# Edge stage of a graph kernel: flat visit loops, the carried sums added by VectorE, a later attention product, and TensorE's first query products ahead of the second gates

## What is computed

```python
q, k, v = x_norm @ Wq.T + bq, x_norm @ Wk.T + bk, x_norm @ Wv.T + bv
dk = silu(edge_attr @ Wdk.T + bdk)
dv = silu(edge_attr @ Wdv.T + bdv)
attn = sum(q[dst] * k[src] * dk, axis=1)
attn = silu(attn) * cosine_cutoff(edge_weight)
agg = segment_sum(v[src] * dv * attn[:, None], dst)
out = x + agg @ Wo.T + bo
```

## Time and profile before

| | |
|---|---|
| median of 3 runs | 2702.92 us (2702.91 to 2708.73) |
| the profiled execution | 2704.13 us |
| its span, first to last instruction | 2702.6 us |
| PE busy, share of the span | 2347.1 us, 87% |
| DVE busy | 2231.1 us, 83% |
| ACT busy | 1899.4 us, 70% |
| POOL busy | 1725.5 us, 64% |

### The profile page before, as it was taken

The page is one execution under the profiler, slowest core; times in us unless marked ns, Lnnn a source line. Parts: engine busy times, 40 slices in busy tenths (PEclk is TensorE's granted clock), DMA queues, the critical chain, the costliest instruction groups (busy, mean ns, idle before and its releaser), DMA issues. The chain is left out here.

```text
span 2702.6 us, 55102 instructions
## 1 busy us (share of the span) xinstructions
PE 2347.1 (87%) x12558; PEld 1931.7 (71%) x12559; DVE 2231.1 (83%) x6310; ACT 1899.4 (70%) x4106; POOL 1725.5 (64%) x1829
## 2 busy tenths in 40 slices
PE   5446686999999999999999999999999999999975
PEld 4323344888888777887778788787778888887864
DVE  4276667998988888898989898898889899898965
ACT  1234334878878777887778777778787888887844
POOL 3343205777777777777777777777776777777723
PEclk8768788999999999999999999999999999999987
DMA  9646536999999999999999999999898999999943
GB/s 298 183 71 164 167 133 192 271 268 275 270 268 271 266 265 266 268 273 263 267 264 268 270 270 267 269 272 267 262 272 263 270 274 269 272 269 270 268 151 116
DMA packets 318259, 662.33 MB, mean 245 GB/s; under 512 B 79334, under 2 KB 131666, under 8 KB 318224
## 3 DMA queue, kind: packets, MB, share of 16 engines
q0 software_dynamic: 137824, 446.91, 57.6%
q1 hardware_dynamic: 172272, 205.20, 25.8%
q10 hardware_dynamic: 8128, 9.90, 1.1%
HBM read 602.50 MB, written 59.30 MB: 245 GB/s over the span
## 5 line engine op out<-in xcount | busy, mean ns | idle before, releaser
L966 POOL DMA_INDIRECT e_kv<-kv_tab,e_idx x1604 | 1565.9, 976 | 602.9 <-issue 475.7
L1089 ACT ACTIVATE e_gate_ps<-e_gate_ps 128x1024 f32<-128x1024 f32 x802 | 811.6, 1012 | 431.9 <-PE e_gate_ps L1022 431.2
L1161 DVE TENSOR_TENSOR e_gated<-e_kv,e_gate_ps 128x1024 f32<-128x1024 f32 x804 | 974.4, 1212 | 16.8 <-DMA e_kv<-kv_tab,e_idx 15.8
L1006 PE MATMUL e_sum_ps<-e_gated,e_weighed_hot 128*128 128x256 f32 x3232 | 837.7, 382 | 99.4 <-issue 97.2
L1021 PE MATMUL e_gate_ps<-wd_hi_lo,e_high 128*128 128x512 f32 x1604 | 745.3, 465 | 31.1 <-DVE e_gated L1161 30.5
L1006 PEld LDWEIGHTS e_sum_ps<-e_gated,e_weighed_hot 128*128 128x128 f32 x3232 | 583.1, 190 | 195.4 <-issue 114.9
L1022 PE MATMUL e_gate_ps<-wd_bias,e_low 128*128 128x512 f32 x1604 | 634.6, 396 | 0.0
L1171 DVE CUSTOM_DVE_ANT_0 e_gated<-e_gated,e_q_ps 128x256 f32<-128x256 f32 x1608 | 603.3, 410 | 2.9 <-PE e_q_ps L1041 2.1
L1099 ACT ACTIVATE e_weighed_hot<-e_hot,e_attn 128x128 f32<-128x128 bf16 x1612 | 524.3, 399 | 0.5 <-DVE e_attn L1183 0.5
L1040 PE MATMUL e_q_ps<-e_q_win,e_hot_t 128*128 128x256 f32 x1604 | 401.0, 283 | 11.9 <-issue 10.9
L1041 PE MATMUL e_q_ps<-e_q_win,e_hot_t 128*128 128x256 f32 x1604 | 397.6, 281 | 0.0
(11 more groups left out here) (145 smaller groups left out, 1632.8 us busy)
## 6 DMA issues: line engine op xcount, KB each, us to landing
e_attr<-attr_groups_dram SPq DMA_DIRECT2D x800, 128.0 KB
e_kv<-kv_tab,e_idx POOLq DMA_INDIRECT x1604
e_q_win<-q_tab SPq DMA_DIRECT2D x100, 256.0 KB
sum_tab<-e_sums SPq DMA_DIRECT2D x102, 128.0 KB
e_prior<-sum_tab SPq DMA_DIRECT2D x101, 128.0 KB
q_tab<-l_q_out SPq DMA_DIRECT2D x50, 256.0 KB, 6.0
kv_tab<-l_kv_out SPq DMA_DIRECT2D x50, 256.0 KB, 6.2
xt_tab<-xt_out SPq DMA_DIRECT2D x50, 132.0 KB, 3.6
```

Of the source, the lines that this page charges most:

```text
L966: pool.indirect_dma_start(kv[:, k, :], None, kv_tab, bass.IndirectOffsetOnAxis(ap=idx[:, k:k + 1], axis=0)).then_inc(kv_landed[k // G][k % ...
L1006: last = nc.tensor.matmul(sum_ps[:, 0:H], weighed_hot[:, c % 2, k, :], gated[:, c * G + k, H:2 * H], start=(c == 0 and k == 0), stop=False)
L1089: nc.scalar.activation(gate_ps[:, 2 * p:2 * p + 2, :], gate_ps[:, 2 * p:2 * p + 2, :], ACT.Silu).then_inc(silu_ready[s][p], 1)
L1161: nc.vector.tensor_tensor(gated[:, pair(s, p), :], kv[:, pair(s, p), :], gate_ps[:, 2 * p:2 * p + 2, :], ALU.mult).then_inc(gated_ready[s] ...
```

## The change

All engines but SP and DVE walk one flat loop over all visits; its length, `total`, is computed once by DVE in the set-up. DVE and SP keep the nested loops, since they need the block and the window. PE steps its wait registers ahead of the visit's last `gather_q`. The product with the identity leaves PE, `take_sums` leaves ACT, and DVE adds the carried rows to the sums in one instruction in group 3, which then waits for the landing of `e_prior`. `attend(c)` moves behind `gate_rows(c, 1)`. In group 0, `e_place` is made behind `gate_rows(0, 0)`, and `one_hot(0)` behind `dot_rows(0, 0)`. `one_hot` and the second `gate_rows` get waits of their own, which were implied before. On PE, `gather_q(c, 0)` moves in front of `gates(c, 1)`. SP's stream is as before.

```diff
+                    then(nc.vector.tensor_copy(spread[:], spread_i[:]))
+                    then(nc.vector.tensor_reduce(further[:], spread[:], AX.X, ALU.add))
+                    nc.vector.tensor_scalar(total[:], further[:], float(BLOCKS), None, ALU.add)
...
+    def of_last(self, c, lag):
+
+        assert c >= lag
+        return self.prev
...
+        def all_visits(eng):
+            return eng.value_load(total[0:1, 0:1], min_val=BLOCKS, max_val=BLOCKS * -(-N // P))
...
-                with pool.Fori(0, BLOCKS) as t:
-                    n = visits(pool, t)
-                    with pool.Fori(0, n):
-                        gather_half(0)
-                        gather_half(1)
-                        visit.step()
+                with pool.Fori(0, all_visits(pool)):
+                    gather_half(0)
+                    gather_half(1)
+                    visit.step()
...
-                                                start=(c == 0 and k == 0), stop=False)
-                    if c == GROUPS - 1 and p == 1:
-                        pe.wait_ge(prior_landed, visit.now16)
-                        last = nc.tensor.matmul(sum_ps[:, 0:H], ident[:], prior[:], start=False, stop=True)
+                                                start=(c == 0 and k == 0), stop=(c == GROUPS - 1 and k == G - 1))
...
-                with pe.Fori(0, BLOCKS) as t:
-                    n = visits(pe, t)
-                    with pe.Fori(0, n):
-                        for c in range(GROUPS):
-                            segment_sum(c, 0)
-                            gates(c, 0)
-                            segment_sum(c, 1)
-                            turn_hot(c)
-                            gates(c, 1)
-                            gather_q(c, 0)
-                            gather_q(c, 1)
-                        visit.step()
+                with pe.Fori(0, all_visits(pe)):
+                    for c in range(GROUPS):
+                        segment_sum(c, 0)
+                        gates(c, 0)
+                        segment_sum(c, 1)
+                        turn_hot(c)
+                        gather_q(c, 0, visit.of)
+                        gates(c, 1)
+                        of = visit.of
+                        if c == GROUPS - 1:
+                            visit.step()
+                            of = visit.of_last
+                        gather_q(c, 1, of)
...
-                def take_sums():
-                    act.wait_ge(summed[GROUPS - 1], visit.prev)
-                    act.wait_ge(stored, visit.now16)
-                    nc.scalar.copy(sums[:], sum_ps[:, 0:H]).then_inc(sums_ready, 1)
-
...
+                with act.Fori(0, all_visits(act)):
+                    for c in range(GROUPS):
+                        silu_of_dot(c)
+                        round_attr(c)
+                        silu(c, 0)
+                        weigh(c)
+                        copy_hot(c)
+                        silu(c, 1)
+                    visit.step()
...
-                    if p == 0:
-                        dve.wait_ge(silu_ready[s][p], visit.of(c, 2))
+                    dve.wait_ge(silu_ready[s][p], visit.of(c, 2))
...
+                    dve.wait_ge(weighed_ready[c][1], visit.prev)
...
+                def take_sums():
+
+                    dve.wait_ge(stored, visit.now16)
+                    dve.wait_ge(go, 1)
+                    dve.wait_ge(prior_landed, visit.now16)
+                    dve.wait_ge(summed[GROUPS - 1], visit.prev)
+                    nc.vector.tensor_tensor(sums[:], sum_ps[:, 0:H], prior[:], ALU.add).then_inc(sums_ready, 1)
...
-                        dve.wait_ge(hot_ready[GROUPS - 1], visit.prev)
-                        nc.vector.tensor_scalar(place[:], dst_f[:, bass.ds(t * BLOCK_TILES, BLOCK_TILES)], window_f[:, bass.ds(t, 1)],
-                                                steps[:, bass.ds(r, 1)], ALU.subtract, ALU.subtract).then_inc(place_ready, 1)
                         for c in range(GROUPS):
                             gate_rows(c, 0)
+                            if c == 0:
+                                dve.wait_ge(hot_ready[GROUPS - 1], visit.prev)
+                                nc.vector.tensor_scalar(place[:], dst_f[:, bass.ds(t * BLOCK_TILES, BLOCK_TILES)], window_f[:, bass.ds(t, 1)],
+                                                        steps[:, bass.ds(r, 1)], ALU.subtract, ALU.subtract).then_inc(place_ready, 1)
+                                dot_rows(c, 0)
+                                one_hot(c)
+                            else:
+                                one_hot(c)
+                                dot_rows(c, 0)
+                            gate_rows(c, 1)
                             attend(c)
-                            one_hot(c)
-                            dot_rows(c, 0)
-                            gate_rows(c, 1)
                             low_attr(c)
+                            if c == GROUPS - 1:
+                                take_sums()
                             dot_rows(c, 1)
```

More of the change, by code:

```diff
@@ L425, in gnn_kernel @@
         edge_stage(nc, dict(
[L426 removed]
+            ident_bf=ident_bf, iota=iota, steps=steps, src_tiles=src_tiles, dst_f=dst_f, cut=cut, window_f=window_f, walk=walk, total=total,
             wd_hi_lo=wd_hi_lo, wd_bias=wd_bias, q_tab=q_tab, kv_tab=kv_tab, sum_tab=sum_tab, attr_groups=attr_groups,
@@ L830, in edge_stage @@
 def edge_stage(nc, shared):
-    ident, ident_bf, iota, steps, src_tiles, dst_f, cut, window_f, walk, wd_hi_lo, wd_bias = (
-        shared[n] for n in ("ident", "ident_bf", "iota", "steps", "src_tiles", "dst_f", "cut", "window_f", "walk", "wd_hi_lo", "wd_bias"))
+    ident_bf, iota, steps, src_tiles, dst_f, cut, window_f, walk, total, wd_hi_lo, wd_bias = (
+        shared[n] for n in ("ident_bf", "iota", "steps", "src_tiles", "dst_f", "cut", "window_f", "walk", "total", "wd_hi_lo", "wd_bias"))
     q_tab, kv_tab, sum_tab, attr_groups, NP, N, BLOCKS = (
@@ L1030, in turn_hot, with gather_q @@
                     last.then_inc(turned[c], 1)
-                def gather_q(c, p):
+                def gather_q(c, p, of):
                     s = slot(c, 1)
                     if p == 0:
-                        pe.wait_ge(hot_t_ready[s], visit.of(c, 1))
+                        pe.wait_ge(hot_t_ready[s], of(c, 1))
                         if s == 0:
                             pe.wait_ge(q_landed, visit.now16)
-                    pe.wait_ge(dotted[slot(c, 2)][p], visit.of(c, 2))
+                    pe.wait_ge(dotted[slot(c, 2)][p], of(c, 2))
                     for k in (2 * p, 2 * p + 1):
@@ L1062, in _ @@
                             gates(c, p)
-                            gather_q(c, p)
+                            gather_q(c, p, visit.of)
             @block.scalar
@@ L1106, in copy_hot @@
                     nc.scalar.copy(hot_t[:, c % 2, :, :], hot_ps[:, 0:G, :]).then_inc(hot_t_ready[c], 1)
-                def take_sums():
-                    act.wait_ge(summed[GROUPS - 1], visit.prev)
-                    act.wait_ge(stored, visit.now16)
-                    nc.scalar.copy(sums[:], sum_ps[:, 0:H]).then_inc(sums_ready, 1)
                 act.wait_ge(dve_ready, 1)
                 nc.scalar.preload_act_table(ACT.Silu)
[L1115 to L1118, removed]
-                            silu_of_dot(c)
-                            round_attr(c)
-                            silu(c, 0)
-                            weigh(c)
-                            copy_hot(c)
-                            if c == GROUPS - 1:
-                                take_sums()
-                            silu(c, 1)
-                        visit.step()
+                with act.Fori(0, all_visits(act)):
[7 more added lines that the diff above has]
+                    visit.step()
                 for c in range(GROUPS - 1):
@@ L1133, in _ @@
                     weigh(c)
-                take_sums()
             @block.vector
             def _(dve):
-                visit = Visits(dve, "dve_e", "cur prev now32 late32")
+                visit = Visits(dve, "dve_e", "cur prev now16 now32 late32")
                 preset(dve, low_ready, 0)
```

5 lines of the change are left out of this document (4 added, 1 removed).

## The result

The changed kernel is slower: 2770.05 us median of 6 runs (2750.78 to 2778.16), where the kernel before took 2702.8 us beside it (6 runs, 2692.15 to 2708.73). The ratio is 1.0249, with a 95% interval from 1.021 to 1.0288. The profiled execution is the longest of the six, with a span of 2776.4 us, against 2702.6 before.

A forecast was written before the change was run, and what follows sets the result against it. PE was taken to set the pace at 21.51 us a visit; fixed steps of 17.12 plus a 3.70 landing gave 20.82. With 0.63 saved a visit, 62 us, the forecast was 2641 us, range 2600 to 2706.

The forecast's parts named there:

- rival C: Landing of `e_q_win` bounds the loop and lengthens to 4.9 us under denser gathers: 22.0 us a visit, 2753 us; chance 0.12.
- The landing: Group 1: `e_q_win` lands 3.70 us after issue, and PE's early query products wait for it.
- The fixed part: PE's visit apart from the landing of `e_q_win`: 17.12 us.
- DVE is slack: DVE needs 20.0 us a visit with its added sum and 0.3 us loop turn, less than PE, so costs nothing.
- The turn of the loop on PE: Between last query product and next visit's first sum: flat loop saves 0.80 us a visit, 0.13 stays.
- the new stall: PE in group 1, before the first query products: 1.3 to 1.4 us each visit, total wait some 100 to 140 us.
- The idle at `e_sum_ps`: PE's idle in front of its sums was to fall from 73 us to under 20.
- The DMA share: Busy share of the DMA engines in the edge loop, 93% before, was to be 0.95 or more.
- The third sign: The prediction would be wrong if DVE waited for key and value rows (`e_kv`) more than 30 us.
- A: Gathers and DMA engines take back 0.2 to 0.35 us a visit through late key and value rows: 2661 to 2690 us; chance 0.17.
- B: Load of `e_q_win` lands earlier or is hidden, saving 1.2 us a visit until POOL bounds it: 2585 us; chance 0.08.
- D: No gain: PE's loop turn stays, or DVE's 20.0 us of work and new place hold PE; 2703 to 2712 us; chance 0.13.

The follow-up runs named there:

- e3: The kernel before with only the new order, first query products ahead of the second gates in all groups: 2859.65 us, 1.06 of before.
- e2: The changed kernel with the old order of second gates and first query products in group 1 alone: 2650.2 us, 0.9823 of before.
- e6: The kernel before with flat loops on PE, ACT and POOL and nothing else, on a slower chip: 0.9856 of before there.
- e8: e2 with PE's two nested loops back, on a slower chip: 0.9513 of before there.
- e4: The changed kernel with twelve unread products on PE in group 1, between transposes and first query products: 2728.17 us, 1.0104 of before.

## Why the prediction was wrong

It said 2641 us, range 2600 to 2706, with 0.75 for faster. It came to 2770, outside the range, on the side of rival C. The sum was 20.82 us a visit. The measured visit is 22.28 us in the mean of 99, 1.46 more, and three terms make this up. One was sized too low, and two were put at nothing.

- **The landing: +0.55.** I took 3.70 and it was 4.25 (3.96 and 4.83 in the two kinds of visits). The mechanism, a sum of fixed part and landing, held (slope 0.92); the size was too low. Rival C named this, with the mean near 4.9 and through denser gathers on fuller DMA engines. The direction is right, the reason is not shown: the landing is 4.1 to 4.25 us in all five kernels with an edit that ran on chips at 2700 us, `e3` among them, while the engines' share in the loop was 0.88 (after), 0.86 (`e3`) and 0.94 (`e2`). How full the engines are does not set it, neither over the loop nor just then: in the 3.5 us behind the issue their share is 0.92 in before and 0.84 in after. The Trainium skill's rule for C ("DMA: Bandwidth & Descriptors", section Latency and other measured facts: HBM's latency grows under load) doesn't explain it in this form, since the load was lower in after. What does set it stays open.
- **The fixed part: +0.42.** I had 17.12 and visits with a steady clock show 17.54. The step that failed is that DVE is slack. PE's timeline, cut at the first sums of each group, shows where it went (means in us; 99 visits of each kernel):

  | kernel, visits | group 0 | group 1 | group 2 | group 3 |
  |---|---|---|---|---|
  | before, 99 | 4.88 | 5.53 | 4.84 | 6.26 |
  | after, clock stays, 67 | 5.41 | 6.46 | 4.82 | 4.81 |
  | after, clock falls, 32 | 5.40 | 8.35 | 5.38 | 4.81 |

  Group 3 gave 1.45, a little more than I took off it (4.81 against 4.97). But group 0, which the sum left as it was, grew by 0.53. DVE's own turn of the nested loop, which I took at 0.3 us and left off the path, is 0.61 us between its last dots and the next gate rows; `gates(0, 0)` on PE waits for those gate rows. DVE's timeline of after at the turn:

```profile
1506.07 0.42 DVE L1169 CUSTOM_DVE_ANT_0 e_gated<-e_gated,e_q_ps 128x256 f32<-128x256 f32 x1
...
1507.10 1.22 DVE L1159 TENSOR_TENSOR e_gated<-e_kv,e_gate_ps 128x1024 f32<-128x1024 f32 x1 [0.61 <-issue]
1508.24 0.34 DVE L1210 TENSOR_SCALAR e_place<-dst_f,window_f,steps 128x16 bf16 x1
```

  The same turn in before, on DVE and on PE:

  ```profile
  1508.24 0.29 DVE L1202 TENSOR_SCALAR e_place<-dst_f,window_f,steps 128x16 bf16 x1 [0.32 <-issue]
  1508.45 1.21 DVE L1161 TENSOR_TENSOR e_gated<-e_kv,e_gate_ps 128x1024 f32<-128x1024 f32 x1
  ...
  1510.35 0.58 PE L1021 MATMUL e_gate_ps<-wd_hi_lo,e_high 128*128 128x512 f32 x1
  ```

  In before the gate rows end at 1509.66, 0.69 us ahead of the gates: that was the margin. In after they end at 1508.32, and PE's gates start at 1508.47, 1.23 us behind their sums (1507.24), where in before it was 0.75 us (1509.60 to 1510.35). Over all visits the two are 1.21 and 0.75. So some 0.5 us of what the flat loop saved on PE came back as a wait in front of the next gates: as long as PE turned slowly, DVE's turn lay under PE's. This is read from the two traces; the runs that were to show it by their times (`e6`, `e8`) fell on the other chips. The waits view had shown me only how little PE waited for DVE there, not by how little DVE was ahead. I had priced DVE's line at 20.0 us a visit against 20.8 and stopped there; the margin to look at was the one at the turn.
- **The clock: +0.50.** Nothing in the prediction spoke of it. The earlier trace rows show it at 1.00 all through the loop, and I let it stand for the new kernel, in which PE would stand 1.3 to 1.4 us in each visit by my own sum, and more in the visits with late landings. In 32 of 99 visits the fixed part is 19.10 instead of 17.54: 32/99 x 1.56 = 0.50. `e4` takes it away and gets some 40 us back, where 0.50 x 99 is 50. The Trainium skill ("TensorE: Matmul & The Clock Gate", section Terms) prices a throttled stretch at its length times the share of pulses left out; for the 109 us at half rate that is an estimate of 55 us, a little above the 50 of the table and the 40 of `e4`.

0.55 + 0.42 + 0.50 is 1.47, against the 1.46 to be explained. One small reading was off as well and is in none of the three: the transposes of the earlier trace rows end at 1517.15 + 0.39 = 1517.54, not at 1517.35, so that a landing of 3.7 us meant a stall of 1.2 us, not 1.3 to 1.4.

**What held.** The turn of the loop on PE is gone, wholly: from the last query product of a visit to the next sum it is 0.12 us (0.13 more was to stay, so the saving is over the 0.80 taken). The identity's product is gone, the wait at `e_attn` too, and the new stall is in group 1, in each visit. It was forecast at 100 to 140 us and is 170.6. The idle at `e_sum_ps` went as forecast. The savings came to 0.89 together (`e3` against after), not 1.36; most of the difference, 0.47, is DVE's turn again (`gates(0, 0)` start 0.75 us behind their sums in `e3`, 1.21 in after).

**The signs named ahead.** The DMA share was to rise to 0.95 or more and fell to 0.88, and the period is over 21.4: both say that the prediction fell. The third sign, late key and value rows, stayed low in after; it appeared in `e2`, where PE is fast enough.

**The other rivals.** A (the transfers take part back) was priced at 0.2 to 0.35 us a visit on top of a gain. Its signs are in `e2`, another kernel than the one it was made for: landings of 4.1 us and key and value rows late three times as often, at 2650 us. B (an early landing) found no support: none of these five has a mean under 4.1. The prediction's 2.6 us for this size is an estimate from a fit that the Trainium skill ("DMA: Bandwidth & Descriptors", section Anatomy of one DMA) gives for DMAs on GpSimd's path; this load is issued by SP, so the fit was stretched to it, and 3.7 to 4.25 was measured among the gathers. C's 2753 us is the price nearest to the result, but by luck in part: its landing of 4.9 was not reached in the mean, and two terms that it did not have make up the rest. D's second half, DVE as the holder, is the 0.42, through its turn and not through its 20.0 us of work.

The point where I chose wrong is the one where I took 3.7 with a break-even at 4.4 and gave C 0.12. With the real fixed part the break-even was 21.51 - 17.54 = 3.97 us, a quarter of a microsecond over the mean I had read, and the loss beyond it is steeper than 1 to 1, because the clock fell behind most of the longest stalls.

## What to carry to other kernels

Before work is moved away from between a load's issue and its first use, take the distribution of the landing, not its mean, and ask what the stall costs beyond its own length: on PE stalls of 1.9 to 2.9 us were followed by a halved clock in 32 of 99 visits. Where one engine's loop turn is removed, look at the others' turns, since they may have lain under it. A reordering that is good in three of four groups (13 us here) can lose in the fourth (115 us), so it is applied group by group, where the data are there already.

## What the runs showed of the hardware

- The granted clock fell from 2.4 to 1.2 GHz within 1.4 us of the end of a stall of 1.9 to 2.9 us, in a loop in which PE is busy 91% of the time, and came back after 3.4 us; 32 times in 99 visits. Stalls of up to 2.6 us also passed without it. Products without a use in the gap held it at 2.4 GHz and made the kernel faster (`e4`, 1.0104 against 1.0249).
- A load of 256 KB issued by SP among gathers took 3.7 us to land in the kernel before and 4.1 to 4.25 in the five others on chips at 2700 us, without a clear relation to the DMA engines' mean share (0.93 in before, 0.86 to 0.94 in the others).
- Chips of one kind ran the same kernel at 2700 us and, four others, at 3809 to 3941 us, and the change has opposite signs on them: +2.5%, and -4.6% on the one of the four where it ran. Why after gains so much there is open; the order of group 1 costs 1.2% there as well.
